# An LSTM step whose two halves are stacked alike: gate sums in PSUM, work moved between the vector engine, the scalar engine and GpSimd

## What is computed

```python
def lstm_scan(x, h0, Wx, Wh, b):
    xW = jnp.einsum('ntd,dg->ntg', x, Wx) + b
    def step(carry, xw_t):
        prev_h, prev_c = carry
        a = xw_t + prev_h @ Wh
        i = sigmoid(a[:, :H]); f = sigmoid(a[:, H:2*H])
        o = sigmoid(a[:, 2*H:3*H]); g = tanh(a[:, 3*H:])
        next_c = f * prev_c + i * g
        next_h = o * tanh(next_c)
        return (next_h, next_c), next_h
...
x = x + lstm_scan(x, cond_1024, Wx, Wh, b)
# second layer: conv and two projections of x, softplus and tanh,
# state = decay * state + dt * b_t * u_t over t, (c_t * state) @ Wo + bo
x = x + second_layer(x, cond_1024)
```

## Time and profile before

| | |
|---|---|
| median of 3 runs | 1887.65 us (1887.31 to 1887.77) |
| span of the profiled execution | 1887.5 us |
| first add of A (step 0) / last (step 511) | 45.83 us / 1871.93 us |
| PE busy | 1806.9 us (96%) |
| DVE busy | 1387.4 us (74%) |
| ACT busy | 1120.3 us (59%) |
| POOL busy | 340.0 us (18%) |
| granted PE clock | 0.996 of full speed, 9 or more tenths in every slice |

### The profile page before, as it was taken

How to read it: one execution, slowest core, us unless ns; L and a number is a source line. 1 busy time by engine, 2 the same in 40 slices (tenths; PEclk the granted TensorE clock), 3 DMA queues, 4 the chain that set the end, 5 groups by cost and what they waited for, 6 DMA issues and landing times.

```text
span 1887.5 us, 124428 instructions
## 1 busy us (share of the span) xinstructions
PE 1806.9 (96%) x52834; PEld 1418.6 (75%) x52834; DVE 1387.4 (74%) x7266; ACT 1120.3 (59%) x4565; POOL 340.0 (18%) x1544
## 2 busy tenths in 40 slices
PE   6888999999999999999999999999999999999987
PEld 3666777777777777777777777777777787888875
DVE  8787667777776777767777776777767777777776
ACT  5555565665655656566565655656556565656564
POOL 1111111111111111111111111111111111111111
PEclk9999999999999999999999999999999999999999
DMA  6111111111111111111111111111112111211110
GB/s 236 54 46 36 48 48 44 51 53 48 50 52 44 57 46 54 49 45 59 46 51 55 49 50 48 57 41 54 54 38 66 44 48 54 60 38 56 44 35 25
DMA packets 112292, 100.75 MB, mean 53 GB/s; under 512 B 20225, under 2 KB 86069, under 8 KB 110710
## 3 DMA queue, kind: packets, MB, share of 16 engines
q1 hardware_dynamic: 111448, 90.70, 15.8%
q10 hardware_dynamic: 288, 2.10, 0.3%
HBM read 50.77 MB, written 41.94 MB: 49 GB/s over the span
## 4 chain that ended last, share of the span: by engine, by line
PE 76%; ACT 9%; DVE 8%; issue 2%; POOL 2%; DMA 1%; SPq 0%; DVEq 0%; ACTq 0%
PE recA L562 28%; PE recB L569 17%; PE pw L521 13%; PE pbc L646 13%; ACT act L851 4%; DVE tr L974 4%; ACT recA L777 3%; DVE pre L983 2%; POOL h L488 2%; DVE hz L1009 2%; PE pw L505 1%; ACT tc L866 1%; PE pu L619 1%; PE po L666 1%; DMA wpk<-in_L_cond_Wh_dram 1%
## 5 line engine op out<-in xcount | busy, mean ns | idle before, releaser
L851 ACT ACTIVATE act<-pre 128x64 f32<-128x64 f32 (+1 forms) x1024 | 255.6, 250 | 709.5 <-DVE pre L983 701.8
L569 PE MATMUL recB<-wlo,hz 128*32 128x128 f16 x16352 | 577.0, 219 | 0.4 <-issue 0.3
L569 PE MATMUL recB<-whi,hz 128*32 128x128 f16 x16352 | 576.8, 219 | 0.2 <-issue 0.2
L562 PE MATMUL recA<-whi,hz 128*16 128x256 f16 x8176 | 515.3, 274 | 54.2 <-DVE hz L1009 46.0
L562 PE MATMUL recA<-wlo,hz 128*16 128x256 f16 x8176 | 511.9, 273 | 0.0
L569 PEld LDWEIGHTS recB<-whi,hz 128*32 128x32 f16 x16352 | 437.5, 97 | 10.0 <-issue 0.4
L569 PEld LDWEIGHTS recB<-wlo,hz 128*32 128x32 f16 x16352 | 437.5, 97 | 3.0 <-issue 0.7
L562 PEld LDWEIGHTS recA<-whi,hz 128*16 128x16 f16 x8176 | 199.9, 88 | 282.5 <-DVE hz L1009 264.4
L974 DVE STREAM_TRANSPOSE tr<-recA 128x256 f32<-128x256 f32 x512 | 230.2, 450 | 228.4 <-PE recA L562 227.2
L646 PE MATMUL pbc<-yt,wpk 128*128 128x256 f32 (+1 forms) x1216 | 332.6, 381 | 0.0
L488 POOL TENSOR_TENSOR h<-osc,tc 128x16 f32<-128x16 f32 x1024 | 228.2, 223 | 451.0 <-ACT tc L866 451.0
(11 more groups left out here) (162 smaller groups left out, 2120.7 us busy)
## 6 DMA issues: line engine op xcount, KB each, us to landing
xw_rows<-xs SPq DMA_DIRECT2D x128, 256.0 KB, 2.4
seed<-xw_rows SPq DMA_DIRECT2D x1008, 32.0 KB, 2.0
xn<-in_x_dram SPq DMA_DIRECT2D x32, 256.0 KB
out_dram<-ot SPq DMA_DIRECT2D x32, 256.0 KB, 3.1
seed<-in_L_cond_Wh_dram ACTq DMA_DIRECT2D x2, 1024.0 KB, 6.9
wpk<-in_L_cond_Wh_dram SPq DMA_DIRECT2D x2, 1024.0 KB, 12.1
wlo<-in_L_cond_Wx_dram SPq DMA_DIRECT2D x2, 1024.0 KB, 13.5
xs<-in_L_cond_Wx_dram SPq DMA_DIRECT2D x1, 1024.0 KB, 9.7
```

The source lines that it names most:

```text
L562: ins = pe.matmul(rec[0][32 * j:32 * j + 2 * NB, 0:256].rearrange("p (c f) -> p c f", c=2), h[:, 2 * NB:4 * NB], w[:, k, :, :].rearrange(" ...
L569: ins = pe.matmul(rec[1][32 * j:32 * j + 32, 0:128], h[:, 2 * NB * (1 - c):2 * NB * (1 - c) + 32], w[:, k, 4 * (2 + c) + j, :], start=Fals ...
L851: act_eng.activation(act[q][:, q:G, :].rearrange("p g n -> p (g n)"), pre[q][:, q:G, :, :].rearrange("p g c b -> p (g c b)"), ACT.Tanh, sc ...
```

## The change

Both halves are now laid out as half B was: 32 rows, 128 columns. `sums` is one code for the four chunks, so every step has 32 quads of 128 columns (before: 8 of 256 and 16 of 128); the PE order by k and chunk stays the same in columns. The transpose of A has 128 columns and not 256. The sums of high and low rows, `pre`, are written by DVE into free columns of the same PSUM banks (`rec0`, `rec1`) and read there by ACT; B's gate o alone goes to `preo` in SBUF. On POOL, (o + 1) of B takes the place of A's float32 h; on DVE, `full` (A's float32 h) is added ahead of `high` A, and so ahead of cell B; `opened` leaves ACT, and seeds B moves ahead of B's gate o. The seeds lie in DRAM in the order in which SBUF wants them: 8 transfers of 64 KB for eight steps and not 16 of 32 KB (6 for steps 2 to 7, not 24), while the way out writes 512-byte pieces and not 2 KB ones. The banks `px` and `pu` become one, with waits of PE on `s_usb`, `s_wev` and `s_xev` that keep their uses apart. Two of the planner's numbers near the end move (20 to 22, 17 to 16).

```diff
-        tr = [sb("tr0", [128, 2, G, 4, NB]), sb("tr1", [128, G, 2, 2, NB])]
-        pre = [sb(f"pre{h}", [128, G, 2, NB]) for h in range(2)]
-        act = [sb(f"act{h}", [128, G + 1, 2 * NB]) for h in range(2)]
-        ifgate, gc = (act[0][:, 0:2, :], act[1][:, 2:4, :]), (act[0][:, 3:5, :], act[1][:, 1:5:3, :])
-        prod = [sb(f"prod{h}", [128, 2, 2 * NB]) for h in range(2)]
-        tc = [sb(f"tc{h}", [128, 2 * NB]) for h in range(2)]
-        osc = [sb(f"osc{h}", [128, 2 * NB]) for h in range(2)]
+        tr = [sb(f"tr{q}", [128, WIDTH[q] // 32, 2, 2, NB]) for q in range(Q)]
+        act = [sb(f"act{q}", [128, G + 1, WIDTH[q] // 8]) for q in range(Q)]
+        prod = [sb(f"prod{q}", [128, 2, WIDTH[q] // 8]) for q in range(Q)]
+        tc = [sb(f"tc{q}", [128, WIDTH[q] // 8]) for q in range(Q)]
+        osc = [sb(f"osc{q}", [128, WIDTH[q] // 8]) for q in range(Q)]
+        preo = sb("preo", [128, 2, NB])
...
+        pre = [rec[q][:, WIDTH[q]:WIDTH[q] + WIDTH[q] // 2].rearrange("p (g n) -> p g n", g=G) for q in range(Q)]
...
+        def scratch_of(g, q):
+            return scratch[g % 2, 65536 * GROUPS[q][0]:65536 * (GROUPS[q][-1] + 1)].rearrange("(s t r f) -> s t r f", s=8, t=TS, r=2 * NB)
+        def seed_rows(eng, g, q, z, p):
+            return eng.dma_start(seed[:, z, p, OFF[q]:OFF[q] + WIDTH[q]],
+                                 scratch_of(g, q)[:, TS // 2 * z + p, :, :])
...
-                sync.dma_start(scratch[g % 2, c, :, :], xs[:, c, :]).then_inc(s_rows[c], 16)
-            def rows_back(g, c, z):
-                if c == 0:
-                    if 2 * g + z >= 2:
-                        sync.wait_ge(s_seed[1], TS * (2 * g + z - 1) - 2)
-                    else:
-                        sync.wait_ge(s_wlo, z + 1)
-                sync.wait_ge(s_rows[c], 16 * (g + 1))
-                back = scratch[g % 2, c, :, :].rearrange("(t q) (j f) -> j q t f", q=2 * NB, j=4)
-                row, col = ((0, 128 * (c % 2)), (2 * NB * (c % 2), 0))[c // 2]
-                for j in range(4):
-                    sync.dma_start(seed[32 * j + row:32 * j + row + 2 * NB, z, :, c // 2, col:col + 128],
-                                   back[j, :, TS // 2 * z:TS // 2 * z + TS // 2, :]).then_inc(s_seedin[z], 16)
+                            sync.wait_ge(s_seed0[p], 16 * Q)
+                to = scratch_of(g, group_of[c])
+                if len(GROUPS[group_of[c]]) == 2:
+                    sync.dma_start(to[row_of[c]::2, :, :, :].rearrange("j t r f -> (t r) j f"),
+                                   xs[:, c, :].rearrange("p (j f) -> p j f", j=4)).then_inc(s_rows[c], 16)
...
+            def rows_back(g, q, z):
+                if 2 * g + z >= 2:
+                    sync.wait_ge(s_seed[q], TS * (2 * g + z - 1) - 2)
+                else:
+                    sync.wait_ge(s_wlo, z + 1)
+                for c in GROUPS[q]:
+                    sync.wait_ge(s_rows[c], 16 * (g + 1))
+                for p in range(TS // 2):
+                    seed_rows(sync, g, q, z, p).then_inc(s_seedin[z], 16)
...
             for t in range(T):
                 pool.wait_ge(s_tg[0], t + 1)
-                pool.tensor_scalar(osc[0][:, :], act[0][:, 2, :], 1.0, SC, ALU.add, ALU.mult).then_inc(s_os[0], 1)
-                for q in range(2):
-                    pool.wait_ge(s_tc[q], t + 1)
-                    pool.wait_ge(s_os[q], t + 1)
-                    if t % HS == 0 and t and q == 0:
-                        pool.wait_ge(s_yadd, t // HS)
-                    pool.tensor_tensor(h32[:, 2 * q:2 * q + 2, t % HS, :],
-                                       osc[q][:, :].rearrange("p (c b) -> p c b", c=2),
-                                       tc[q][:, :].rearrange("p (c b) -> p c b", c=2), ALU.mult).then_inc(s_h32[q], 1)
+                pool.tensor_scalar(osc[0][:, :], act[0][:, 3, :], 1.0, SC, ALU.add, ALU.mult).then_inc(s_os[0], 1)
+                pool.wait_ge(s_tgo, t + 1)
+                pool.tensor_scalar(osc[1][:, :], act[1][:, 3, :], 1.0, SC, ALU.add, ALU.mult).then_inc(s_os[1], 1)
+                if t % HS == 0 and t:
+                    pool.wait_ge(s_yadd, t // HS)
+                pool.wait_ge(s_tc[1], t + 1)
+                pool.wait_ge(s_os[1], t + 1)
+                pool.tensor_tensor(chunks(h32, 1)[:, :, t % HS, :], by_chunk(osc, 1), by_chunk(tc, 1),
+                                   ALU.mult).then_inc(s_h32[1], 1)
...
+                    if g >= 2:
+                        pe.wait_ge(s_wev, KC)
+                        before = sum(u_when[i][0] < x_base(g) for i in range(NP))
+                        if before:
+                            pe.wait_ge(s_usb, before)
+                ins = pe.transpose(pxu[:, 128 * k:128 * k + 128], xn[:, g % 2, 128 * k:128 * k + 128], ident[:, :])
...
+            def recur(t, c, k):
+                for w in (whi, wlo):
+                    ins = sums(hz[(t - 1) % 2][:, k, :], c, w, k)
+                return ins
+            def sums(h, c, w, k):
+                q, end = group_of[c], k == KC - 1
+                if WIDTH[q] == 128:
+                    for j in range(4):
+                        ins = pe.matmul(rec[q][32 * j:32 * j + 32, 0:128],
+                                        h[:, 2 * NB * (1 - row_of[c]):2 * NB * (1 - row_of[c]) + 32], w[:, k, 4 * c + j, :],
+                                        start=False, stop=end, skip_group_check=True)
+                    return ins
...
+                    pe.wait_ge(s_h[0], t + 1)
+                    if t > 1:
+                        pe.wait_ge(s_seed[0], t - 1)
                     recur(t, 0, 0)
+                    recur(t, 1, 0)
                     recur(t, 0, 1)
-                    recur(t, 1, 0, (0,))
+                    recur(t, 1, 1)
+                    if t > 1:
+                        pe.wait_ge(s_seed[1], t - 1)
+                    recur(t, 2, 0)
+                    pe.wait_ge(s_h[1], t + 1)
                     recur(t, 0, 2)
+                    recur(t, 1, 2)
                     recur(t, 0, 3)
-                    recur(t, 1, 0, (1,))
-                    recur(t, 1, 1)
-                    recur(t, 1, 2)
-                    recur(t, 1, 3)
+                    recur(t, 1, 3).then_inc(s_rec[0], 1)
+                    recur(t, 3, 0)
+                    recur(t, 2, 1)
+                    recur(t, 3, 1)
+                    recur(t, 2, 2)
+                    recur(t, 3, 2)
+                    recur(t, 2, 3)
+                    recur(t, 3, 3).then_inc(s_rec[1], 1)
...
-            def gates(t, q):
+            def gates(t, q, slots):
                 act_eng.wait_ge(s_add[q], t + 1)
-                act_eng.activation(act[q][:, q:G, :].rearrange("p g n -> p (g n)"),
-                                   pre[q][:, q:G, :, :].rearrange("p g c b -> p (g c b)"), ACT.Tanh, scale=gain).then_inc(s_tg[q], 1)
-            def opened(t):
-                act_eng.wait_ge(s_tgo, t + 1)
-                act_eng.activation(osc[1][:, :], act[1][:, 0, :], ACT.Copy, bias=SC, scale=SC).then_inc(s_os[1], 1)
+                act_eng.activation(act[q][:, 0:slots, :].rearrange("p g n -> p (g n)"),
+                                   pre[q][:, 0:slots, :].rearrange("p g n -> p (g n)"), ACT.Tanh, scale=gain).then_inc(s_tg[q], 1)
             def gate_o(t):
                 act_eng.wait_ge(s_addo, t + 1)
-                act_eng.activation(act[1][:, 0, :], pre[1][:, 0, :, :].rearrange("p c b -> p (c b)"), ACT.Tanh,
+                act_eng.activation(act[1][:, 3, :], preo[:, :, :].rearrange("p c b -> p (c b)"), ACT.Tanh,
...
-                    gates(t, 0)
+                    gates(t, 0, 4)
                     if 1 < t + 1 < T:
                         seeds(t + 1, 0)
-                    gates(t, 1)
+                    gates(t, 1, 3)
                     tanh_c(t, 0)
-                    gate_o(t)
-                    opened(t)
-                    tanh_c(t, 1)
                     if 1 < t + 1 < T:
                         seeds(t + 1, 1)
+                    gate_o(t)
+                    tanh_c(t, 1)
...
-            def add(t, q):
-                dve.wait_ge(s_tr[q], t + 1)
-                if q:
-                    dve.tensor_tensor(pre[1][:, 1:G, :, :], tr[1][:, 1:G, :, 0, :],
-                                      tr[1][:, 1:G, :, 1, :], ALU.add).then_inc(s_add[1], 1)
-                else:
-                    dve.tensor_tensor(pre[0][:, :, :, :].rearrange("p g c b -> p c g b"), tr[0][:, :, :, 0, :],
-                                      tr[0][:, :, :, 1, :], ALU.add).then_inc(s_add[0], 1)
...
+            def add(t):
+                dve.wait_ge(s_tr[0], t + 1)
+                dve.tensor_tensor(pre[0][:, :, :].rearrange("p g (c b) -> p g c b", c=2), tr[0][:, :, :, 0, :],
+                                  tr[0][:, :, :, 1, :], ALU.add).then_inc(s_add[0], 1)
+            def add_gif(t):
+                dve.wait_ge(s_tr[1], t + 1)
```

(45 more changed lines are left out.)

214 lines of the change are left out of this document (91 added, 123 removed).

## The result

The changed kernel takes 2161.54 us against 1887.71 us: ratio 1.143, 95% interval 1.1395 to 1.1472. The forecast was 1905, with a range of 1876 to 1936. The sign was right, the size not: 274 us slower and not 17.

The account below looks back on a forecast made before the run. The prediction took a ring of hand-overs through PE, DVE, ACT and POOL as the bound, growing from 3.535 to 3.58 us. Over 390 steps and some disturbed ones, less 2.2 for transfers, +17.3 gave 1905 us, range 1876 to 1936.

Parts of the forecast that it names:

- PE, no change: PE's matmuls: two small quads cost what one large did, so A's and B's ends stay, to 0.01 us.
- Cover is not needed: PE's 32 quads: no allowance made; slower pairs of weights and products than in half B would cost each quad.
- the small form of A is slower on PE: Rival on PE: 0.007 for each of 16 quads, 0.11 us on the ring, +48, 1936 us; chance 0.08.
- the ring: Cycle of hand-overs through PE, DVE, ACT and POOL that sets a step: forecast 3.535 + 0.035 + 0.01 = 3.58 us.
- o + 1 of B on POOL: POOL, before h32 of B: own-result hand-over 0.04 us, h32 at G + 1.045 (bounds 1.005 to about 1.10), 0.035 later.
- G: Start of gates B on ACT, 903.53 in the trace before; the prediction timed B's branch from it.
- Adds and gates in PSUM: ACT gates reading PSUM: 0.04 us off each; DVE adds writing PSUM: +0.01, bounds -0.04 to +0.04, only add B on the path.
- Seeds A and transpose A: ACT seeds A, 461 to 353 ns, gains 0; DVE transpose A, 0.45 to 0.32 us, passes on 0.01 of 0.13.
- B's branch: From gates B to h32 of B: cell B queued behind `high` A at G + 0.53, where it stood at G + 0.50.
- Transfers: Seed transfers at the start: waits at steps 1 and 7 go, 2.2 us off; smaller way-out pieces hidden in the loop.
- The sum: Whole run: 17.6, 0.3 and 1.6 us from lengthened steps, less 2.2: +17.3, so 1905 us.

Follow-up runs that it names:

- a_wide: Changed kernel with half A's products back at 16 rows by 256 columns, 96 pairs a step, chunk 1 lacking its recurrent part: 1957.3 us, 1.036 of before.
- a_wide_act: a_wide with (o + 1) of B back on ACT and seeds B back behind the tanh of c of B: 1908.4 us, 1.010 of before.
- b_split: Kernel before with each of half A's 256-column products issued as two of 128, nothing else touched: 2158.1 us, 1.140 of before.
- c_psum: Kernel before with the gate sums alone moved to PSUM, B's gate o in SBUF: 1878.6 us, 0.992 of before.

## Why the prediction was wrong, point by point

**PE, no change: the step that failed.** Its times are right. The stalled step's quads still come every 0.055, and a_wide, with the old form, has the same transposes of A and B 0.782 apart. What it says next, "Cover is not needed", is wrong. It costed the 32 added pairs by how fast PE takes them, and not by how fast they reach PE. The rival "the small form of A is slower on PE" was a rate of the same kind and would have shown quads longer than 0.055; it isn't what happened. (Its sum, too, is short: 0.11 on the ring comes on top of the 0.045 and not in its place, so it should have read about 1953 and not 1936. And of the ten quads that the prediction puts between 904.45 and 905.02, the kernel before has six, four large and two small; the 0.57 us are measured and stand.) The page of before had the two numbers: 415 packets for 52834 matmuls, thus 0.81 packet a step of 3.57 us, one in 4.4 us. They weren't read. Nor were the few stalls with no releaser that its trace has. That 3.9 us is the least that a packet can be had in couldn't be read off them, but they bounded nothing from above either: an edit that raises the need of a resource by 31% wanted a rival with that resource, and the range its end.

**o + 1 of B on POOL: mis-sized.** The route was right to 0.02 (gate o at G + 0.50 for 0.52 forecast, (o + 1) at + 0.79 for 0.80). The hand-over from POOL's own result to its next instruction was taken as 0.04 with a bound of some 0.10; it is 0.15 (1103.69 + 0.20 to 1104.04). DVE gets the same result after 0.10 (1103.99). The neighbour from DVE was a poor one, and the bound was too near. In the ring it is 0.10 of the 0.155, some 45 us of the 49 that a_wide_act gives back. In the changed kernel itself it costs next to nothing, since the supply sets the step there (4.116 us in the mean, and 4.107 in b_split without it).

**Adds and gates in PSUM: right.** Forecast 0.04 off the gates and 0.01 on the adds; measured 0.034 and 0.014 (0.009 for A) in the rows, and 0.007 for add B on the path. (Add B's row misses by 0.005 the 0.01 that the prediction's own sign allowed it.) By the Trainium skill (Perfetto Trace Analysis, Optimizing Scalar/DVE Operations), with 60 ns on SBUF and 125 on PSUM for VectorE, add B would hold its engine 0.065 longer. The section says of its figures that they are engine-busy times and that a profiled instruction shows about twice as much; the prediction left that out, and by it the row would be 0.13 longer. The rows here don't agree: 0.014 in the row's duration, and DVE's next instruction starts 0.125 behind add B in c_psum and 0.126 in the kernel before. For ScalarE the section has 93 against 51, so 0.042, and about twice that in a row; gates B's row is 0.034 shorter, near the single figure.

**Seeds A and transpose A: right, as far as rows show it.** Neither was tried by itself. Product A starts 0.24 behind transpose B (1102.54 after 1102.30) as forecast.

**B's branch: right.** Cell B directly behind `high` A at G + 0.52 (0.53 forecast). With POOL's part taken away the ring is 3.563, where the same working gives 3.535 + 0.03 + 0.01.

**Transfers: about right, hidden by the rest.** Step 1 lasts 4.02 in a_wide and 5.13 before, step 7 3.85 and 4.15; with the ring's growth taken off some 1.7 us were gained, as 2.2 were forecast. In the changed kernel a stall of PE takes the place of the first one.

**The sum.** Had only POOL's 0.10 been mis-sized, the forecast would have been some 50 us short, 1957 for 1905, itself outside the range. The rest comes from a resource that no case had, and that resource alone makes 2158 (b_split). That the sign was right is in part luck: the 17 us were to come from the ring, which by itself makes 68 (a_wide), while b_split makes nearly the whole of the 274 with the ring of before, out of a term that the sum put at nothing.

## What to carry to other kernels

Count the instructions of an engine in each turn of the loop, and read the "instruction" queue in the page's third part beside them, before an edit that cuts an operation into smaller ones: here 111 pairs of weight load and matmul in a step of 3.54 us cost 0.6% over 103, 119 cost 3.2% and 135 cost 14.0%, though PE had the time to execute them. Idle time "issue" in the midst of equal instructions is the sign. And where a result passes from an engine to itself or to a neighbour on the critical ring, take its hand-over from a row of that engine and that kind of operation, or leave the bound wide.

## What the runs showed of the hardware that I had not expected

- PE's instructions came in packets of 16 KB, one for 127 matmuls with their weight loads, and in the mean of a run could not be had more often than once in about 3.9 us (single starts lie as near as 3.2 us): 4.107 us a step with a ring of 3.54, 4.116 with 3.69, 4.163 with 3.89, all with 135 pairs a step. By the changed kernel's 192 stalls it is a trip with one packet under way at a time: 1.27 us in the median from PE's going on to the next packet's start, and 2.56 from a packet's start to PE's going on, 1.1 of which the packet itself takes. That is read from the trace and wasn't tested by a run; why the next packet isn't sent for earlier stays open.
- A tensor-scalar operation on GpSimd (0.20 us) was taken up 0.15 us after its end by GpSimd and 0.10 after it by DVE, where the product's result (0.22 us) is taken up by DVE 0.03 after its end. The profile's ends on GpSimd are rough; from start to start it is 0.35 us to GpSimd's next instruction, where the prediction's terms give 0.245.
- A cell update of 16 columns on DVE took 0.20 us and not 0.17 while a GpSimd operation ran beside it. POOL's row ends at 905.70, cell B's at 905.73 after a start at 905.53, so it wasn't held back for the whole of it. The Trainium skill (SBUF — State Buffer, Who interferes with whom) says that a VectorE instruction with two inputs in SBUF contends with a GpSimd instruction that reads SBUF; by that rule the two rows agree (`cell` has both inputs in SBUF), with 0.03 us as the price that they show. But h32 of A on GpSimd reads SBUF too and runs beside the same cell B in the kernel before, and there no such price is seen (178 ns against 175 with GpSimd idle), so the price depends on something that no run here varied.
